# Moving three weight loads up SyncE's queue, and a context transpose ahead of the value matmuls, in a cross-attention and mixture-of-experts kernel

## What is computed

```python
x = x + xattn(layernorm(x), ctx)         # 16 batches x 256 tokens, width 256, 16 heads, 77 context rows
    q = x @ Wq + bq;  k, v = split(ctx @ Wkv + bkv)
    out = softmax(q k^T / 4) v;  return out @ Wp + bp
x = x + ffn(layernorm(x))
    xf = layernorm(x) * g + b
    scores, idx = top_k(xf @ router, 2);  gate = softmax(scores)      # 8 experts
    out += gate[e] * expert_e(xf)        # layernorm, x1 = .@W1+b1, x2 = clip(.@W2+b2), (x1*silu(x2)) @ Wo + bo, clips
```

## Time and profile before

| what | us |
|---|---|
| median of 3 runs | 1046.07 |
| lowest and highest run | 1041.0, 1052.43 |
| the profiled execution's own time | 1046.82 |
| its span, first to last instruction | 1045.0 |

### The profile page before, as it was taken

One profiled execution on the slowest core, in us unless ns is written; L12 is line 12 of the kernel. 1 busy time (PEld: TensorE's weight loads), 2 busy tenths in 40 slices (PEclk: granted clock), 3 DMA queues, 4 the chain that ended last, 5 costly groups with the idle time before them and its releaser, 6 DMA issues.

```text
span 1045.0 us, 19526 instructions
## 1 busy us (share of the span) xinstructions
PE 956.4 (92%) x6372; PEld 845.6 (81%) x6372; DVE 788.2 (75%) x1775; ACT 689.3 (66%) x1354; POOL 422.8 (40%) x653
## 2 busy tenths in 40 slices
PE   4999999999968898999999999999999999999883
PEld 3788878788757776788989898989898988889873
DVE  2578887876855776877878888878788878788881
ACT  2667776766654663676868686868677777677761
POOL 4455666757744535441250414132323232232222
PEclk9899999999885898999999999999999999999996
DMA  6232333333252355544655565555555655455553
GB/s 142 40 60 49 81 67 79 83 68 82 56 149 72 109 198 169 157 102 114 190 132 183 127 178 137 152 162 147 151 164 130 182 129 174 126 157 146 154 178 114
DMA packets 135069, 132.97 MB, mean 127 GB/s; under 512 B 60256, under 2 KB 119344, under 8 KB 134832
## 3 DMA queue, kind: packets, MB, share of 16 engines
q1 hardware_dynamic: 121520, 113.66, 36.9%
q0 software_dynamic: 13440, 17.97, 9.5%
HBM read 105.32 MB, written 25.88 MB: 126 GB/s over the span
## 4 chain that ended last, share of the span: by engine, by line
PE 59%; DVE 13%; issue 9%; ACT 8%; DMA 4%; another core or an unknown queue 3%; SPq 2%; POOL 1%; ACTq 0%; DVEq 0%; POOLq 0%
PE bank L1726 25%; PE bank L1756 13%; PE bank L1598 5%; PE bank L1538 4%; PE bank L1520 3%; DVE wl L1398 3%; DMA raw<-in_W 2%; PE bank L1575 2%; ACT wh L909 2%; DVE yo L1447 1%; PE bank L1619 1%; DVE xl L1404 1%; PE bank L1705 1%; PE bank L1565 1%
## 5 line engine op out<-in xcount | busy, mean ns | idle before, releaser
L730 POOL DMA_INDIRECT out_rows<-yo,token x72 | 125.9, 1748 | 438.4 <-ACT yo L968 423.7
L1726 PE MATMUL bank<-xh,wh 128*128 128x512 f32 (+1 forms) x768 | 268.2, 349 | 20.6 <-DVE hid L1429 15.3
L1726 PE MATMUL bank<-xl,wh 128*128 128x512 f32 (+1 forms) x768 | 263.0, 342 | 1.4 <-issue 1.3
L1726 PE MATMUL bank<-xh,wl 128*128 128x512 f32 (+1 forms) x768 | 262.9, 342 | 0.2 <-issue 0.2
L1398 DVE TENSOR_TENSOR wl<-raw,wh 128x1024 fp32r<-128x1024 f32 x148 | 178.3, 1220 | 39.6 <-ACT wh L909 35.3
L1726 PEld LDWEIGHTS bank<-xh,wh 128*128 128x128 f32 x768 | 147.2, 192 | 40.7 <-DVE hid L1429 19.7
L1756 PE MATMUL bank<-wl,hh 128*128 128x256 f32 x576 | 163.5, 284 | 5.3 <-issue 5.3
L1756 PE MATMUL bank<-wh,hh 128*128 128x256 f32 x576 | 164.4, 285 | 3.7 <-DVE yo L1447 3.7
L1756 PE MATMUL bank<-wh,hl 128*128 128x256 f32 x576 | 163.6, 284 | 0.4 <-issue 0.4
L1726 PEld LDWEIGHTS bank<-xh,wl 128*128 128x128 f32 x768 | 147.3, 192 | 19.5 <-issue 1.6
L909 ACT ACTIVATE wh<-raw 128x1024 fp32r<-128x1024 f32 x148 | 152.9, 1053 | 11.1 <-DMA raw<-in_W 11.1
(11 more groups left out here) (160 smaller groups left out, 1862.4 us busy)
## 6 DMA issues: line engine op xcount, KB each, us to landing
raw<-in_W SPq DMA_DIRECT2D x52, 1024.0 KB, 4.9
raw<-in_Wo SPq DMA_DIRECT2D x25, 1024.0 KB
zg<-z_rows SPq DMA_DIRECT2D x12, 520.0 KB, 6.0
xs<-in_x SPq DMA_DIRECT2D x32, 128.0 KB, 2.3
out_rows<-x SPq DMA_DIRECT2D x32, 128.0 KB, 1.8
zg<-z_rows SPq DMA_DIRECT2D x14, 260.0 KB, 3.7
bo_row<-in_bo SPq DMA_DIRECT2D x26, 128.0 KB, 3.5
k_blocks<-k_parts SPq DMA_DIRECT2D x128, 19.2 KB
```

What stands on the lines that cost most here:

```text
L730: e.indirect_dma_start(out=out, out_offset=bass.IndirectOffsetOnAxis(ap=token[j % 4][:, s:s + 1], axis=0), in_=yo[:, s, :], in_offset=None ...
L1726: mm = e.matmul(ps[:, h * cols:(h + 1) * cols], ws[j % 2][:, w, c, m * P:(m + 1) * P], xx[j % 2][:, c, 0:cols], start=(h == 0 and c == 0 a ...
```

## The change

On SyncE's queue, the wait for the early table, the parameters and W2 of tile 0 go from the end of round 28 to its start, and Wo goes from the end of round 30 to before that round's row store. On TensorE the context transposes of an odd round go from the start of its third part to before the value matmuls in the second. On ScalarE the context copy goes from behind the second exponential and the xn computation to before both. Nothing is added or taken out, and the order of claims on the two shared banks is the same.

```diff
@@ sync_program, loop over the rounds
                 nb = i // 2 + 1
                 batch = 0 <= nb < BATCH
+                if i == EARLY_TILES + 8:
+                    e.wait_ge(early_known, 1)
+                    load_expert(0)
+                    load_matrix(0, 1)
                 if 8 <= i + 7 < NT:
                     load_x(i + 7)
                 if batch and i % 2:
                     load_values(nb)
                     if nb + 2 < BATCH:
                         load_ctx(nb + 2)
+                if i == EARLY_TILES + 10:
+                    load_matrix(0, 2)
                 if 0 <= i - 2 < NT:
                     store_x1(i - 2)
                 if batch and i % 2 == 0:
                     store_values(nb)
                     spread_keys(nb)
-                if i == EARLY_TILES + 8:
-                    e.wait_ge(early_known, 1)
-                    load_expert(0)
-                    load_matrix(0, 1)
                 if i == EARLY_TILES + 9:
                     load_matrix(0, 0)
                     wait_puts(EARLY_TILES // 2)
                     load_rows(0)
-                if i == EARLY_TILES + 10:
-                    load_matrix(0, 2)
@@ act_program, round_ops
+                if 0 <= nb + 1 < BATCH and not even:
+                    ctx_t(nb + 1)
                 if 0 <= i < NT:
                     exp_scores(i, 1)
                 if 0 <= i + 4 < NT:
                     make_xn(i + 4)
-                if 0 <= nb + 1 < BATCH and not even:
-                    ctx_t(nb + 1)
@@ pe_program, round_second and round_third
                 if i % 2 == 0 and 0 <= i // 2 - 4 < PAIRS:
                     place_pair(i // 2 - 4)
+                if i % 2 and 0 <= i // 2 + 2 < BATCH:
+                    transpose_ctx(i // 2 + 2)
                 if 0 <= i - 1 < NT:
                     values(i - 1)
 
             def round_third(i):
-                if i % 2 and 0 <= i // 2 + 2 < BATCH:
-                    transpose_ctx(i // 2 + 2)
                 if 0 <= i + 3 < NT:
                     transpose_xn(i + 3)
```

## The result

The changed kernel takes 1063.14 us (median of 4 runs, 1061.26 to 1067.11) against 1046.36 us for the kernel before (4 runs): ratio 1.0159, 95% interval 1.0122 to 1.0196. It is 1.6% slower. That is at the top end of the predicted range of 1026 to 1063: the ratio on the shown median of 1046.07 gives 1062.7. The profiled execution took 1061.26 us with a span of 1059.5, so 14.5 us more span than before.

What follows compares the result with a forecast made beforehand. TensorE, busy 92% of the span, was taken as the bound, so only its idle or low-clock stretches could be won. -6.5 + 11.5 = +5.0 on 1046.82 gave 1051.8 us (1051 against the median); own range 1043 to 1058, whole range 1026 to 1063.

Steps and rivals of the forecast that it cites:

- part B: Context transposes and copy moved earlier in odd rounds: +11.5 us, between -2 and +25.
- part A: Weight loads moved earlier on SP's queue, shortening the wait before round 30's scores: -6.5 us, between -10.8 and -2.9.
- second rival: Odd rounds 13 to 27: each new wait brings a double-length half-clock spell with the values inside; 1065 us, chance 0.18.
- chain L909, L1398, L1086: ScalarE's wait for tile 0's matrix delays VectorE's half, then the subtraction before round 30's scores; 5.4 us to win.
- a wait of 3 us: TensorE's remaining wait before round 30's scores, 305.2 to 308.1, with VectorE late next instead of the transfer.
- 1.1 us taken for the clock: Round 30 after the shortened wait: gain from less half clock, 1.1 taken of up to 5.4 us.
- The row load and the third matrix: Tile 0's rows and Wo share the DMA engines with the second matrix; rows at worst 2.5 us late.
- third rival: The early matrix isn't used, landing late or scores held at 313.54 by something else; part A 0, 1058 us, chance 0.10.
- Part B, the waits: Odd rounds 13 to 27: TensorE's context transposes wait for the logits copy, values behind them; 8 rounds at 0.8, +6.4 us.
- Part B, the clock: TensorE's longer waits in odd rounds bring 3 more half-clock spells at 1.7 us each: +5 us.
- first rival: The late logits copy doesn't matter to TensorE; xf wait and five half-clock spells go, -15.5 us: 1025 us, chance 0.22.
- this case: Odd rounds: if the logits matmuls themselves were late, TensorE wouldn't idle and part B's 0.8 a round would be 0.

Runs made afterwards that it cites:

- second group: Kernel before and changed kernel rerun unchanged, 1042.9 and 1056.16 us (ratio 1.0154); each again with three copies added ahead of the logits copy, 1050.4 and 1070.15 us.
- first pair: Profiles of the kernel before and the changed kernel from the main measurement; medians 1046.36 and 1063.14 us.
- second pair: Profiles of the kernel before and the changed kernel, both rerun unchanged on another occasion; 1042.26 us (one run) and 1056.16 us.
- context alone: Only the context transposes and the context copy moved, weight loads left, against the kernel before at 1027.5 us: 1024.92 us, ratio 0.9977.
- weights alone: Only SyncE's weight loads moved, context transposes and copy left, against the kernel before at 1027.5 us: 1023.27 us, ratio 0.9952.
- fourth group: The changed kernel rerun unchanged against the kernel before at 1043.3 us: 1056.83 us, ratio 1.0131.
- first and third: Two groups: parts of the change run separately (kernel before 1027.5 us); TensorE fill, moved scatters, and weights with ScalarE's copy (kernel before 1024.5 us).
- copy alone: Only ScalarE's context copy moved ahead of the second exponential, against the kernel before at 1027.5 us: 1029.15 us, ratio 1.0.
- first group: Four kernels, each with one part of the change, against the kernel before at 1027.5 us: 1023.27, 1024.92, 1029.15 and 1025.18 us.

## Why the prediction was right in its sign and short in its size

The forecast was +5 us and the measured median is 16.8 us up (13.3 in the second group). It said the change would lose by part B and gain by part A, and both did; the balance was off. The result lies outside the forecast's own range of 1043 to 1058, and it is inside the whole range only because that took in most of the second rival's. Slower by over 1%, as it came out, had been given 0.25, and within 1% 0.50.

- Part A, forecast -6.5 us: the traces have -5.1 and -4.6 at tile 29 and -5.5 at the end of the first pair, the experiment alone -4.9. The chain L909, L1398, L1086 was right, and so was what is late next: VectorE, with a wait of 3.40 us against "a wait of 3 us". The 1.1 us taken for the clock didn't come: behind the 3.40 us wait the 330:340 stretch of the changed kernel ran at 0.50 again. The row load and the third matrix cost nothing that can be seen. The third rival falls.
- Part B, the waits, forecast +6.4 us: after has 12.5 + 1.5 us before L1546, and the 7.0 us before L1632 are gone, so +7.0. The step "the value matmuls covered this wait ... Now nothing does" is what happened in the traces, and the added lateness of the second group made that wait longer and the kernel slower.
- Part B, the clock, forecast +5 us: this is the step that failed, "I take +5, nearest to what rows show". What is left of the 21.0 us is 14, and the stretch's clock, 0.94 to 0.86, holds 12 of them. In the second pair some 10 us are left of 17.6. Both pairs are read from traces, and no experiment measures the clock's share. The term is too small because spells got longer, and not only more: the missing clock of the stretch goes from 9 to 21 us, and in six of the eight rounds of the first pair the half clock reached into the value matmuls, in two through all of them (4.40 us in place of 2.31), where the forecast added three spells of 1.7 us. The second rival had priced part B at 25 us and the whole at 1065, two us from the measured 1063. Its condition, a spell of double length in each of the eight rounds with the values inside it, held in full in only two, so part of its nearness is luck. It still deserved a larger chance: the wait of round 30 in the trace of before had already shown half clock through a whole round with values in it.
- The first rival, 1025 by part B freeing TensorE, is wrong where the copy is late. Where it is prompt its direction may hold, but not its size: -2.4 us, with an interval that reaches zero, instead of -15.5, since there is hardly a wait to free.
- The Trainium skill ("Perfetto Trace Analysis", section "Tensor Engine Instruction (MATMUL, LD_WEIGHTS)") says that a matmul's recorded end is an estimate. So the matmuls themselves might have been late, and part B's waits then free; the prediction named this case. The runs speak against it: with these waits in the trace tile 28 came 17.6 to 21.0 us later and the clock fell, and the same order without them, in the context alone, had a clock of 1.00 and no loss. The wait was real.

## What to carry to other kernels

Before an instruction is moved ahead of a block of work on an in-order engine, look up what the block was covering: the old place of these transposes hid a wait of 2 us for another engine's copy, and no row of the old profile names it as a wait of TensorE. Price a new gap on TensorE by what may run right behind it at half clock, and not by the gap alone. And run a small change on more than one chip: here the same kernel before took 1025 and 1043 us. By the traces of the whole change the context move costs 18 to 21 us beside the slower one, and measured alone it costs nothing beside the faster one, so a verdict from one chip doesn't hold for the other.

## What the runs showed of the hardware

TensorE's signals can reach other engines late, and not on every run. In the profile before, the logits matmuls of round 27 end at 279.28 by their row, and ScalarE, idle, starts on them at 281.96; in the kernel with the weights alone, in a group where the kernel before took 1027.5 us, no copy between 140 and 300 us was late. This went with the chip as far as three chips can tell: all profiles of the second and fourth group, on two chips, had late copies, and none of the first and third, which ran on one chip at different times. The kernel before differed by some 17 us between them. In the profile before, GpSimd's row scatters lie right ahead of the late signal of round 27, but the same scatters ran in the prompt groups without it, so they aren't the cause alone. What is, stays open.

The expert stage has the same pairing. In the profile before, from 402.6 to 410.1 us, beside a row of scatters by GpSimd, TensorE starts nine matmuls at distances of up to 1.9 us with no named wait between them (busy 3.41 of 7.50 us), and ScalarE idles 9.55 us before the copy that follows them (L944). In the copy alone, in the first group, the matmuls of that place start about 0.23 us apart beside the same scatters, and TensorE is busy all the time. The changed kernel has this wait of 9.5 us too, so it doesn't bear on the change; it is the 8 us of difference named above. On the slower chips it isn't only that signals are late: here TensorE's own matmuls start late.

The half clock's coming and its length were not what I had expected either. The old order has six waits of 1.03 us before the xf transposes between 140 and 290 us. The four that end at 165.66, 222.91, 243.09 and 263.65 were followed by the half clock, at 1.8 us of clock in 20 us each, and so was the wait of 0.51 us that ends at 283.97 (0.62 from 284 to 288); the two that end at 146.85 and 204.07 were not. The waits of the new order, 1.8 to 2.4 us for the most part, took the clock of 150 us from 0.94 to 0.86 and doubled the time of the value matmuls in two rounds, but behind the one of 2.33 us, which ended at 214.74, the clock fell only when they were done. So the length of a wait alone didn't decide here whether and when it fell.
